# A shorter fill between pairs of indirect transfers on GpSimd, and all engine orders planned anew for it

## What is computed

```python
x = x + 0.5 * ffn(layernorm(x))      # stage A
x = x + attention(layernorm(x))      # stage B
x = x + 0.5 * ffn(layernorm(x))      # stage C

# ffn
probs = softmax(x @ gate_w.T + gate_b); vals, idx = top_k(probs, 2)
h = relu(x @ w1[e] + b1[e]);  out = h @ w2[e] + b2[e]
sum over the two experts idx of out * vals
# attention
scores = q @ k.T * scale; softmax(scores) @ v; @ Wo.T
```

## Time and profile before

| | us |
|---|---|
| median of 3 runs | 1188.9 |
| lowest and highest | 1188.76, 1192.47 |
| the profiled execution's own time | 1187.95 |
| its span, first to last instruction | 1186.2 |

### The profile page before, as it was taken

One profiled execution on the slowest core, in us unless ns is written; L12 is line 12 of the kernel. 1 busy time (PEld: TensorE's weight loads), 2 busy tenths in 40 slices (PEclk: granted clock), 3 DMA queues, 4 the chain that ended last, 5 costly groups with the idle time before them and its releaser, 6 DMA issues.

```text
span 1186.2 us, 25770 instructions
## 1 busy us (share of the span) xinstructions
PE 1116.0 (94%) x8142; PEld 736.6 (62%) x8142; DVE 720.2 (61%) x2254; ACT 910.1 (77%) x2255; POOL 712.1 (60%) x868
## 2 busy tenths in 40 slices
PE   5989998999999999999999999999999999999896
PEld 3657575676675557566665666666665446657574
DVE  4766468576785557376664686556556646557335
ACT  2339678788897989797898888888888988788431
POOL 3136558674758888028888643886602885268555
PEclk9979998999999999999999999999999999999988
DMA  8074573856645177656565636576732155648872
GB/s 288 2 273 146 176 210 111 257 155 207 205 136 152 45 224 218 174 154 201 173 199 167 180 113 193 154 221 183 210 107 65 39 181 158 184 142 242 256 239 74
DMA packets 159882, 202.05 MB, mean 170 GB/s; under 512 B 16938, under 2 KB 103426, under 8 KB 159747
## 3 DMA queue, kind: packets, MB, share of 16 engines
q1 hardware_dynamic: 144196, 168.90, 46.5%
q0 software_dynamic: 15360, 31.49, 9.1%
q10 hardware_dynamic: 192, 0.02, 0.0%
HBM read 152.50 MB, written 47.84 MB: 169 GB/s over the span
## 4 chain that ended last, share of the span: by engine, by line
PE 70%; ACT 17%; DVE 4%; POOL 4%; issue 3%; DMA 2%; SPq 0%; POOLq 0%; ACTq 0%; DVEq 0%
PE psum L1584 65%; ACT psum L1199 7%; ACT probs L1190 6%; PE psum L1702 2%; POOL Y L1108 2%; DVE neg_m L1538 2%; PE psum L1767 1%; ACT hg L1236 1%; POOL pause L1072 1%; PE psum L1669 1%; ACT xnB L1155 1%; DMA results_C<-ys 1%; DMA xs<-slots_C 1%; DVE neg_hl L1557 0%; PE psum L1662 0%
## 5 line engine op out<-in xcount | busy, mean ns | idle before, releaser
L1538 DVE TENSOR_REDUCE neg_m<-psum 128x1 f32<-128x512 f32 x512 | 317.4, 682 | 153.1 <-PE psum L1584 152.9
L1584 PE MATMUL psum<-nat 32*128 32x512 f32 x2048 | 362.4, 637 | 0.9 <-ACT nat L1266 0.4
L1199 ACT ACTIVATE psum<-psum,neg_m 128x512 f32<-128x512 f32 x512 | 341.0, 680 | 26.5 <-DVE neg_m L1538 25.8
L1190 ACT ACTIVATE probs<-psum 128x512 f32<-128x512 f32 x512 | 266.4, 631 | 42.7 <-PE psum L1584 42.4
L1584 PEld LDWEIGHTS psum<-nat 32*128 32x128 f32 x2048 | 130.5, 184 | 93.4 <-issue 25.5
L1584 PEld LDWEIGHTS psum<-xg_T,wt 128*128 128x128 f32 x1296 | 157.4, 195 | 43.7 <-ACT probs L1190 13.6
L1072 POOL MEMSET pause<- 128x900 f32 x212 | 183.3, 865 | 0.1
L1584 PE MATMUL psum<-xg_T,wt 128*128 128x128 f32 x1296 | 172.5, 283 | 7.9 <-DMA wt<-packed 6.0
L1088 POOL DMA_INDIRECT slots_A<-xnA,posA x120 | 117.6, 980 | 91.0 <-DMA xs<-slots_A 40.9
L1584 PEld LDWEIGHTS psum<-wt,hg 128*128 128x128 f32 x1296 | 151.9, 192 | 31.6 <-ACT psum L1199 11.8
L1108 POOL DMA_INDIRECT Y<-results_C,posC x120 | 115.6, 963 | 90.2 <-issue 69.7
(11 more groups left out here) (190 smaller groups left out, 1382.2 us busy)
## 6 DMA issues: line engine op xcount, KB each, us to landing
wt<-packed SPq DMA_DIRECT2D x324, 320.0 KB
xs<-slots_A SPq DMA_DIRECT2D x36, 256.0 KB
results_A<-ys SPq DMA_DIRECT2D x36, 256.0 KB
xs<-slots_C SPq DMA_DIRECT2D x36, 256.0 KB
results_C<-ys SPq DMA_DIRECT2D x36, 256.0 KB
X<-in_L_attn_x_dram SPq DMA_DIRECT2D x16, 256.0 KB, 7.9
out_dram<-X SPq DMA_DIRECT2D x16, 256.0 KB
packed<-probs SPq DMA_DIRECT2D x1, 2560.0 KB, 8.2
```

The source lines that it names most:

```text
L1190: act.activation(probs[:, kt, j, :], at.banks()[j][:], ACT.Exp).then_inc(a_done, 1)
L1199: act.activation(at.banks()[j][:], at.banks()[j][:], ACT.Exp, bias=neg_m[:, g, n, j:j + 1], accum_out=sums[:, g, n, j:j + 1]).then_inc(S[" ...
L1538: V_.tensor_reduce(neg_m[:, g, n, j:j + 1], at.banks()[j][:], AX.X, ALU.max, negate=True).then_inc(S["r_done"], 1)
L1584: return nc.tensor.matmul(dst, w, m, start=start, stop=stop)
```

## The change

The buffer `pause` has 400 columns, not 900, and line 1072 fills that much. The planner's GAP is 2.95, not 3.4. All numbers of the table of wanted times are other ones, so that every engine's order comes out anew. What each step does, the buffers and their rings, and the division into chunks stay. The order of GpSimd has 213 fills, and had 212.

```diff
-PERIOD, FIRST_B = 54.81, 448.4
...
+PERIOD, FIRST_B = 59.66, 581.43
...
-GAP = 3.4
...
+GAP = 2.95
...
-        pause = sb("pause", [P, 900])
+        pause = sb("pause", [P, 400])
```

More of the change, by code:

```diff
@@ L83, in split_name @@
     return "rsplit" if by_rows(b, g) else "msplit"
-PERIOD, FIRST_B = 54.81, 448.4
[L91 to L99, removed]
-GAP = 3.4
+PERIOD, FIRST_B = 59.66, 581.43
+WANTED = {"norm": -90.89, "scaled": 249.97, "xT": 16.93, ("q", 0): -728.9, ("k", 0): 81.95, ("v", 0): 210.47,
+          ("v", 1): 146.25, ("q", 1): -143.23, ("k", 1): -454.6, "wo": -111.35}
+GROUP_GAP, MAX_PACE, S_FIRST, S_PACE, PV, ADD, SUM = 14.42, 12.71, -292.78, 13.08, -40.83, 62.13, 210.85
+A_LEAD, A_PACE, A_ROUTE, A_NORMS = 13.98, 8.48, 145.42, 3.42
+C_NORM, C_ROUTE, C_FIRST, C_PACE, C_GATHER = 53.42, 39.69, 5.73, 73.5, -7.03
+LOAD_AHEAD, W_AHEAD = -110.28, -62.49
+B_SHIFT = [-301.94, 325, -476.34, -72.53, -82.61, -139.64, -80.46, -112.86, -325, 18.17, -246.86, -381.34, -157.34, -117.31, 87.75, -118.72]
+A_SHIFT = [-207.06, -51.19, -70.9, -104.43, 56.38, 159.45, 6.73]
+C_SHIFT = [27.6, 155.5, 153.37, 156.29, 118.46, -415.5, 388.21]
+GAP = 2.95
 def wanted_attention(b):
```

## The result

Beside each other on one chip, the kernel before took 1192.3 us (median of 10 runs) and the changed one 1195.67 (10 runs, 1192.86 to 1204.67). The ratio is **1.0044, interval 1.0025 to 1.0063**: 0.44% slower where 0.4% faster was forecast. The time lies inside the range of 1175 to 1197, on the wrong side of no change. The profiled execution took 1195.46 us, span 1193.7.

What follows compares the result with a forecast made beforehand. PE, busy 94% of the span, was taken as the bound. Five terms, -3.2 - 2.6 + 3.1 - 4 + 2 = -4.7 us, took the median of 1188.9 to 1184.2 us; range 1175 to 1197.

Steps and rivals of the forecast that it cites:

- the three signs named for being wrong: DVE still waiting for gathers at the end; a second weight stall; attention's last batch after 1118 with the end unchanged.
- The fill: On POOL, a fill of 0.43 us, pairs 2.96 us apart, and 91 us less POOL busy time.
- the opening sentences: POOL mostly has time; the gain must come from the end, stretches where POOL sets a batch's start, and the new order.
- Term 1: Program end: last comb no longer waits for gathers and ends at 1179.9, not 1183.1; -3.2 us, between 0 and -4.7.
- Term 2: PE's stall for weights near the end shrinks from 5.95 to 3.3 us; -2.6 us, from -6 to +3.
- Term 3: One more C11 quad behind the last Wo product costs 4.1 us there, against 1.0 under attention; +3.1 us, or 0.
- Term 4: Early, where POOL sets the pace: batch 2's attention hangs on a comb that comes sooner; -4 us, from 0 to -4.7.
- the first rival: The gain is taken back: PE is the bound, batch 2 waits longer later, term 4 is 0; 1188.2 us, chance 0.20.
- Term 5: Three places where products with `m_rows` directly follow their transpose and wait for the ACT copy; +2 us, from 0 to 2.7.
- The slower loads: Denser gather pairs take DMA turns from the weight loads and slow them; 1187.3 us, chance 0.05.
- The late quad of C10: C10's first quad arrives late and PE stands up to 5 us; 1193.5 us, chance 0.25 with its kind.
- an order with waits that I don't see: The wider kind of the rival of C10's late quad: unseen waits in the new order; chance 0.25 together.

Runs made afterwards that it cites:

- the store ahead: Changed kernel with only the store of C11's last quad moved ahead of C12's weight loads 4 to 7 on SP's queue: ratio 1.0025.
- an experiment of its own: Kernel before with a fill of 400 and C11's quad 4 moved behind the last product with Wo on PE, ACT and DVE: ratio 0.9989.
- the new orders with both moves: Changed kernel; on SP the 2,560 KB load behind C11's last weight loads, C11's last store ahead of C12's weight loads 4 to 7: 0.9971; with fill 100, 0.9953.

## Why the prediction was wrong, point by point

The forecast was 4.7 us less, and it came to 0.44%, some 5 us, more. Terms 1 and 2 failed, both at the end of the program, and the clock had no term. Two of the three signs named for being wrong came: DVE still waits for the gathers at the end, and there is a second stall for weights.

**The fill**: right. 0.45 us, pairs 2.93 apart, POOL 87.7 us less.

**What it is worth**: the opening sentences said that the gain must come from the end, the head and the order. The old orders gained 0.44% from the fills outside the last twelve. I priced only waits of 3 us and more on DVE and passed over the many small ones: of the 24.7 us of line 1503, and the earlier trace rows show 6.8. That a fill also lengthens short DVE instructions I had not seen.

**Term 1 (-3.2)**: the step that failed is "the gathers are no longer late". It moved the twelve pairs by their fills and took their start from the old trace. But the start hangs on C11's last rows, and those on the very stall and quad of terms 2 and 3. The pairs began 11.9 us later. What stands behind it was right for DVE: with the store ahead the comb follows directly. But I took DVE's last work for the end of the program, and there it is POOL's DRAIN behind the last gather, 2.5 us after SP was done. By that path the term is +7.3: 11.9 for the late start less 4.6 for the fills.

**Term 2 (-2.6)**: the step that failed is "so its last quad needs 2.56 + 0.96 = 3.5 MB, about 10 us from the issue", with one stall near 3.3. I had SP issue C11's loads as if nothing held it. Tile 19 waited behind three loads that wait for scatters (6.33 us), and the next tiles came only with the big transfer (3.10 and 0.22). The 2,560 KB stood behind the same three: issued at 1115.87, 6.4 us after the last product with V had ended (1109.48). Measured +3.7, beyond my upper bound of +3, and not at the two places of that bound: both stalls are ahead of C11's products, and C12's first have none. That the second stall with the 0.22 comes to the forecast 3.3 is luck: from the issue of the 2,560 KB to these products it was 13.4 us and not 11.1, and PE came late to them itself. The 1.1 for issue and landing in that sum rests on no row; the 13.1 us of the earlier trace rows run from the issue to the product and hold it already.

**Term 3 (+3.1)**: right in the trace of an experiment of its own, as the difference of two prices that were both 0.6 too low. What it left out: everything that waits for C11's last rows moves too.

**Term 4 (-4)**: batch 2's comb came 10.6 us sooner, at 208.21 where the earlier trace rows has 218.82, and I had said near 215. PE's first products of batch 2 (`psum<-ident,xnB`) came at 218.49 and not 228.88. But the product with Wo of batch 1 slipped from 247 to 271, and that of batch 5 stood at 506 in both: by then the gain was taken back, as the first rival said, and other stretches gained later. The step "batch 2's attention hangs on that comb" failed too. In the old orders with the short fill the comb came at 215.93, without a wait, and PE's first products of batch 2 were no sooner than before: at 231.41, in an execution that was 2.5 us later already at the product with V ahead of them (212.44 and not 209.91). The comb was 5.4 us sooner against that product, and they still stood 1.72 us for ACT's `xnB`, as before. It was the new order that moved them.

**Term 5 (+2)**: the waits came, 0.69 and 0.78 us at single places, 2.1 in all by the groups by line, where before `m_rows` isn't named. What they cost in time no run shows:

```profile
L1584 PE MATMUL psum<-nat 32*128 32x512 f32 x2048 | 359.7, 642 | 3.6 <-ACT m_rows L1215 2.1
```

**The clock**: no term at all. From 900 on the new orders run stretches of bare attention, and the granted clock there is 0.81, which is 2 x 0.19 x 45 = 17 us at half clock:

```profile
900.00:945.00 45.00, 43.35 (x232) 20.96 (x229) 26.08 (x82) 32.45 (x83) 33.49 (x42) 0.81 0.16 52
```

Before, the 100 us from 900 had 0.98, and the earlier trace rows has 0.97 for 64 us without quads, so bare attention alone doesn't explain the 0.81; its cause is open. I had written of this stretch "each worth 3.1 us", in products, and nothing for the clock. The timed runs have a mean clock of 0.964 after, and 0.972 for the kernel before beside the experiments. The stall's own price has the same gap: it costs what PE stands and again half of what it then works at half clock.

**The rivals**: the gain taken back held for the head. The slower loads did not show in the old orders, down to a fill of 100, where PE's waits for weights fell with the fill, 6.0 to 3.4 us. The Trainium skill, "DMA: Bandwidth & Descriptors", section "Queues, rings and completion order", says that engines go round between queues a packet at a time. No run here shows a cost of that at this load. In the new orders with both moves these waits are 5.3 us at 400 columns and 6.1 at 100, one trace each, and the time did not grow. The late quad of C10 did not come: its row at 974.75 has no wait. The kind it stood for, "an order with waits that I don't see", is what happened, at the end and not there.

**Slips in the sums**, none of which turns the forecast: term 1 is said to reach -4.7, but the low end of the range is added up with -3.2 (with -4.7 it is 1173.5 and not 1175.0); and the ten fills ahead of C10's quad are 4.3 us, not 4.7.

## What to carry to other kernels

When a step is moved in an order, follow what hangs on its result to the end of the program before any term further down is priced: here one late load moved a quad, its store, twelve pairs and the end of the program. Look in the trace for what ends the span; it need not be the last instruction that computes. In a queue that issues in order, look at what each entry waits for, not only at its bytes; a small load behind one that waits, or behind a big one, is as late as that. And test a retuned table of orders apart from the knob that it was retuned for: 0.7% of gain by the knob and 1.2% of loss by the table showed as 0.4%, and the knob alone, one number, gives the kernel that is faster than both.

## What the hardware showed that I had not expected

- A 320 KB load issued 1.2 us behind a 2,560 KB one on the same queue served its products 12.2 us after its issue, where such loads, as far as the profile gives their landing, took 3.3 to 6.1 to land (median 4.3); the big one itself took 12.6 from issue to landing, and 9.9 to 12.8 over all 16 traces.
- Within the runs of one kernel the time follows the mean granted clock: 0.6 to 1.0 us more for each 0.001 less, after and in 12 of the 14 experiments (correlation 0.67 to 0.96; 0.3 us and 0.4 in the two with a longer fill in the new orders). By that, two traces of one order whose clocks differ by 0.01 differ by 6 to 10 us. The trace of the old orders with 400 columns, at 0.968, hid its middle gain; the one short in the last twelve only, at 0.979, looked faster than it is. Medians and idle times compare better.
- Indirect instructions kept their 0.95 to 0.98 us and their gaps of 0.27 and 0.30 us at pairs 3.39, 2.93 and 2.70 us apart.
- POOL's DRAIN at the end took 10.84 to 11.02 us in all 16 traces, whatever the fill, and in the nine of the new orders it set the end of the span, 2.0 to 2.5 us behind SP's.
- A fill on POOL holds some short DVE instructions that read and write SBUF: the cast of line 1557 took 0.18 us alone and up to 1.47 where it met a fill of 900 columns, and then ended with it. Some casts were longer beside an indirect instruction too. The long reductions from PSUM (line 1538) had a median of 0.68 us at 900 and at 100 columns alike.
